# Products that nobody reads in TensorE's waits, a shorter root, a second context buffer, and a wait moved to its write

## What is computed

```python
# layer 0
x = x + cross_attention_0(ln(x), ctx, mask0)     # 16 heads of 16, logits tanh(u)*10, keys and values are ctx itself
x = x + self_attention_0(ln(x))                  # 16 heads, q and k normalised per head (rms), softmax over 256 keys
x = x + ternary_linear(ln(x))                    # weights to -1/0/1, rows to 8 bit integers, one 256x256 product
# layer 1
x = x + cross_attention_1(ln(x), ctx, mask1)     # q, k, v projected; softmax over 4096 keys
x = x + causal_attention(ln(x))                  # 16 heads of 64
x = x + ffn(ln(x))                               # latent attention (4 heads), router, top 2 of 8 experts + a shared one
```

## Time and profile before

| | |
|---|---|
| three runs | 779.72, 775.89, 775.08 us, median 775.89 |
| the profiled execution | 776.85 us, of which its span in the trace is 775.1 |
| PE busy | 619.4 us, 80% of the span |
| PE weight loads | 381.6 us, 49% |
| DVE busy | 417.9 us, 54% |
| ACT busy | 464.7 us, 60% |
| POOL busy | 71.7 us, 9% |
| mean granted clock of TensorE | 0.913 of full |
| DMA | 73.41 MB, mean 95 GB/s |

### The profile page before, as it was taken

One profiled execution on the slowest core, in us unless ns is written; L12 is line 12 of the kernel. 1 busy time (PEld: TensorE's weight loads), 2 busy tenths in 40 slices (PEclk: granted clock), 3 DMA queues, 4 the chain that ended last, 5 costly groups with the idle time before them and its releaser, 6 DMA issues. The chain is left out here.

```text
span 775.1 us, 14282 instructions
## 1 busy us (share of the span) xinstructions
PE 619.4 (80%) x4872; PEld 381.6 (49%) x4872; DVE 417.9 (54%) x921; ACT 464.7 (60%) x558; POOL 71.7 (9%) x148
## 2 busy tenths in 40 slices
PE   2696768788878876497369999999998699845997
PEld 1353434444444343275235555555554567634886
DVE  6564541322322314765578898988982436345443
ACT  3896959999999964273036676776776047203010
POOL 3010201000100003000110101111110100000000
PEclk9998979999999985699568999999999599979799
DMA  5877754476443104000622222332220900000000
GB/s 132 217 215 221 247 174 114 129 206 185 121 119 112 48 22 148 0 1 1 222 65 63 86 80 78 86 79 81 85 63 1 336 30 2 1 0 1 1 0 14
DMA packets 52695, 73.41 MB, mean 95 GB/s; under 512 B 10866, under 2 KB 29618, under 8 KB 52658
## 3 DMA queue, kind: packets, MB, share of 16 engines
q1 hardware_dynamic: 51890, 72.19, 31.7%
q10 hardware_dynamic: 768, 0.73, 0.3%
HBM read 58.89 MB, written 12.85 MB: 93 GB/s over the span
## 5 line engine op out<-in xcount | busy, mean ns | idle before, releaser
L1550 DVE TENSOR_REDUCE sb_m_blk<-ps 128x1 f32<-128x512 f32 x256 | 159.6, 684 | 22.1 <-PE ps L1408 20.9
L1359 ACT ACTIVATE sb_probs<-ps 128x1024 f32<-128x1024 f32 x128 | 125.9, 1025 | 52.5 <-PE ps L1438 51.3
L644 ACT ACTIVATE sb_probs<-ps 128x1024 f32<-128x1024 f32 x128 | 124.0, 1017 | 24.9 <-PE ps L690 22.3
L648 ACT ACTIVATE sb_probs<-sb_probs,sb_neg_cap,sb_cap 128x4096 f32<-128x4096 f32 x32 | 121.6, 3801 | 1.1
L707 PE MATMUL ps<-sb_probs,sb_v_st 128*32 128x256 f32 x1024 | 77.0, 398 | 38.3 <-ACT sb_probs L648 38.3
L1408 PE MATMUL ps<-sb_k_st,sb_q_m 96*128 96x512 bf16 x256 | 91.1, 400 | 2.7 <-DVE sb_m_blk L1550 2.1
L690 PE MATMUL ps<-sb_q_st,sb_k_st 112*128 112x256 bf16 x512 | 76.8, 286 | 5.2 <-DMA sb_k_st<-k_parts_l 4.0
L1438 PE MATMUL ps<-sb_q_st,sb_k_st 115*128 115x256 bf16 x512 | 77.7, 275 | 1.4 <-ACT sb_probs L1359 1.4
L690 PEld LDWEIGHTS ps<-sb_q_st,sb_k_st 112*128 112x128 bf16 x512 | 46.4, 101 | 49.4 <-ACT sb_probs L644 23.9
L1454 PE MATMUL ps<-sb_probs,sb_v_st 128*32 128x256 f32 x1024 | 67.4, 384 | 0.2 <-ACT sb_probs L1359 0.2
L1438 PEld LDWEIGHTS ps<-sb_q_st,sb_k_st 115*128 115x128 bf16 x512 | 49.3, 98 | 19.2 <-issue 2.5
(11 more groups left out here) (254 smaller groups left out, 825.1 us busy)
## 6 DMA issues: line engine op xcount, KB each, us to landing
sb_k_st<-k_parts_l SPq DMA_DIRECT2D x223, 64.0 KB, 2.0
sb_k_st<-k_parts_l SPq DMA_DIRECT2D x93, 128.0 KB, 3.1
k_parts_l<-sb_v_proj SPq DMA_DIRECT2D x24, 256.0 KB
k_parts_l<-sb_early SPq DMA_DIRECT2D x48, 128.0 KB
sb_v_proj<-ctxT_blocks SPq DMA_DIRECT2D x8, 512.0 KB, 8.3
sb_early<-ctxT SPq DMA_DIRECT2D x8, 512.0 KB, 3.8
sb_v_rows<-ctx_by_pair SPq DMA_DIRECT2D x7, 512.0 KB, 4.3
sb_k_st<-k_parts_l SPq DMA_DIRECT2D x64, 32.0 KB, 1.7
```

Of the source, the lines that this page charges most:

```text
L644: a.activation(probs[:, j % 2, 4 * g:4 * g + 4, :], scores_bank(g), ACT.Tanh).then_inc(s["tanh"], 1)
L648: a.activation(probs[:, j % 2], probs[:, j % 2], ACT.Exp, bias=k.neg_cap[:, 0:1], scale=k.cap[:, 0:1]).then_inc(s["exp"], 1)
L1359: sc.activation(probs[:, g], scores_bank(g), ACT.Exp).then_inc(s["exp"], 1)
L1550: v.tensor_reduce(k.m_blk[:, b, q, blk:blk + 1], k.ps[:, m_bank(m_turn_of(idx)), :], AX.X, ALU.max).then_inc(s["m_read"], 1)
```

## The change

- `rsqrt` takes the first guess y, and then t = v*y*y and y times a polynomial of t, written as two quadratic factors: eight instructions where there were ten, two of them issued beside another one.
- `keep_busy(k, n, bank)` issues n matmuls of 128x512 in float32 (ones, and the columns of the output weights `w1_o`) to a PSUM bank that nobody reads then. It stands ahead of waits of TensorE: 5 in `update_pe` where a norm follows (stages two and four), 8, 4 and 8 in stage two, 4 ahead of the flag's load in stage three, 2, 9 and 5 in stage four. It waits for nothing itself.
- A second context buffer `ctx_two` takes the block of pair 1, the normalised rows `xn` and `xnT` of the later stages lie in the same memory. The copies are issued in another order: pair 1 right behind the second key load for pair 1, pair 2 where that of pair 1 stood. `next_ctx(2)` for pair 3 stays.
- VectorE's wait for the stored blocks 6 and 7 goes from the loop's entry into `v_rows` for j = 2 of the loop.

```diff
 RSQRT_MAGIC = float(0x5F3759DF)
+RSQRT_POLY = (0.27406409802012394, (-0.9034915739820695, 1.7067952240054962), (-4.242021545393216, 5.265408709688565))
...
     k.rs_t = k.sb("rs_t", [P, 64])
-    k.xn = k.sb("xn", [P, QT, D])
-    k.xnT = k.sb("xnT", [P, KT, S])
+    k.rs_z = k.sb("rs_z", [P, 64])
+    k.rs_w = k.sb("rs_w", [P, 64])
+    k.ctx_two = k.sb("ctx_two", [P, KT, CBLK])
+    k.xn = k.ctx_two[:, 0, :].rearrange("p (t d) -> p t d", t=QT)
+    k.xnT = k.ctx_two[:, 1, :].rearrange("p (t q) -> p t q", t=KT)
     k.o_nat = k.sb("o_nat", [P, QT, D])
...
-    v, y, t = k.rs_v[:, 0:n], k.rs_y[:, 0:n], k.rs_t[:, 0:n]
+    v, y, t, z, w = (buf[:, 0:n] for buf in (k.rs_v, k.rs_y, k.rs_t, k.rs_z, k.rs_w))
     vec = k.nc.vector
+    (a1, b1), (a2, b2) = RSQRT_POLY[1:]
     link(vec.tensor_scalar(y.bitcast(I32), v.bitcast(I32), -0.5, RSQRT_MAGIC, ALU.mult, ALU.add))
-    for _ in range(3):
-        link(vec.tensor_tensor(t, y, y, ALU.mult))
-        link(vec.scalar_tensor_tensor(out=t, in0=t, scalar=-0.5, in1=v, op0=ALU.mult, op1=ALU.mult))
-        link(vec.scalar_tensor_tensor(out=y, in0=t, scalar=1.5, in1=y, op0=ALU.add, op1=ALU.mult))
+    link(vec.tensor_tensor(t, y, y, ALU.mult), vec.tensor_scalar(z, y, RSQRT_POLY[0], None, ALU.mult))
+    link(vec.tensor_tensor(t, t, v, ALU.mult))
+    link(vec.scalar_tensor_tensor(out=w, in0=t, scalar=a1, in1=t, op0=ALU.add, op1=ALU.mult),
+         vec.scalar_tensor_tensor(out=y, in0=t, scalar=a2, in1=t, op0=ALU.add, op1=ALU.mult))
+    link(vec.scalar_tensor_tensor(out=z, in0=w, scalar=b1, in1=z, op0=ALU.add, op1=ALU.mult))
+    link(vec.scalar_tensor_tensor(out=y, in0=y, scalar=b2, in1=z, op0=ALU.add, op1=ALU.mult))
...
         "proj", "v_copied", "kd_ops", "kd_split", "q_rows", "q_turned", "q_first", "q_stack", "keep",
-        "v_first", "ctx_pair", "first_hi", "first_res", "first_mid")}
+        "v_first", "ctx_pair", "two_in", "first_hi", "first_res", "first_mid")}
     k_in = [k.sem(f"a_k_in{j}") for j in range(4)]
...
                 load_first(1, j)
+            sp.dma_start(k.ctx_two[:, :, :], ctx_blocks[:, :, CBLK:2 * CBLK]).then_inc(s["two_in"], 16)
             store_block(2)
...
                 store_kd1(0, j)
-            next_ctx(0)
+            sp.wait_ge(s["proj"], 4)
+            sp.dma_start(k.ctx_blk[:, :, :], ctx_blocks[:, :, 2 * CBLK:3 * CBLK]).then_inc(s["blk_in"], 16)
             load_first(1, 3)
...
                 sp.wait_ge(s["scores"], 16 + 4 * (j + 1))
-                if j == 3:
-                    next_ctx(1)
                 load_first(2, j)
...
-            def project(it, j, first):
+            def project(it, j, first, second=False):
+                ctx = k.ctx_two if second else k.ctx_blk
                 if j == 0:
-                    pe.wait_ge(s["blk_in"], 16 * (it + 1))
+                    if second:
+                        pe.wait_ge(s["two_in"], 16)
+                    elif first:
+                        pe.wait_ge(s["blk_in"], 16)
+                    else:
+                        pe.wait_ge(s["blk_in"], 16 * it)
                     if first:
...
                     for c in range(KT):
-                        last = t.matmul(k.ps[:, bank, :], k.wk1[:, c, j * P:(j + 1) * P], k.ctx_blk[:, c, :],
+                        last = t.matmul(k.ps[:, bank, :], k.wk1[:, c, j * P:(j + 1) * P], ctx[:, c, :],
                                         start=(c == 0), stop=(c == KT - 1))
...
                         for c in range(KT):
-                            last = t.matmul(k.ps[:, bank, m * D:(m + 1) * D], k.ctx_blk[:, c, ch * P:(ch + 1) * P], k.wv1[:, c, :],
+                            last = t.matmul(k.ps[:, bank, m * D:(m + 1) * D], ctx[:, c, ch * P:(ch + 1) * P], k.wv1[:, c, :],
                                             start=(c == 0), stop=(c == KT - 1))
...
                     if not first:
-                        project(it, j, False)
+                        project(it, j, False, fresh)
                     elif j >= 2:
...
-            def v_rows(it, j):
+            def v_rows(it, j, over_parts=False):
                 dve.wait_ge(s["proj"], 4 * it + j + 1)
+                if over_parts:
+                    for n in (6, 7):
+                        dve.wait_ge(k.sem(f"k0_stored{n % 2}"), blocks_stored(n))
                 v.tensor_tensor(k.v_proj[:, bass.ds(4 * it + 2 * (j - 2), 2), :],
...
                     else:
-                        v_rows(it, j)
+                        v_rows(it, j, block_of is None and j == 2)
                     if block_of is not None:
...
             body(1, FIRST_LATE)
-            for n in (6, 7):
-                dve.wait_ge(k.sem(f"k0_stored{n % 2}"), blocks_stored(n))
             with dve.Fori(2, H // 2) as it:
...
+def keep_busy(k, n, bank):
+
+    for _ in range(n):
+        k.nc.tensor.matmul(k.ps[:, bank, :], k.ones_sq[:, :], k.w1_o[:, :, :].rearrange("p t n -> p (t n)"), start=True, stop=True)
+
+
 def update_pe(k, pe, tag, src, n_k, w, turn, norm=True):
...
     if norm:
+        keep_busy(k, 5, 6)
         pe.wait_ge(k.sem(tag + "_xn"), QT)
...
             t.matmul(k.ps[:, 7, 0:1], k.ones_sq[:, :], k.w_sum[:, :], start=True, stop=True).then_inc(k.sem("c_w_total"), 1)
+            keep_busy(k, 8, 6)
             pe.wait_ge(k.sem("b_qkn"), QT)
...
             last.then_inc(k.sem("b_qkT"), 1)
+            keep_busy(k, 4, 6)
             pe.wait_ge(k.sem("b_kT"), 1)
...
+            keep_busy(k, 8, 6)
             pe.wait_ge(k.sem("c_aq"), 1)
...
+            keep_busy(k, 4, 6)
             masked = pe.value_load(k.masked_i[0:1, 0:1], min_val=0, max_val=1)
...
             small_pe(k, pe, causal)
+            keep_busy(k, 2, 0)
             pe.wait_ge(k.sem("e_oT"), 1)
...
+            keep_busy(k, 9, 0)
             pe.wait_ge(k.sem("f_xn"), QT)
...
+            keep_busy(k, 5, 0)
             pe.wait_ge(k.sem("g_xn"), QT)
```

## The result

The changed kernel takes 749.44 us (median of four runs, 745.07 to 750.28) against 775.49 for the kernel before: the ratio is 0.9638, 95% interval 0.9599 to 0.9677. The profiled execution took 750.28 us, its span is 748.6.

What follows compares the result with a forecast made beforehand. Bounds: ScalarE's pace and two gaps in stage one, then VectorE's chain in TensorE's waits and half clock behind them. -4.9 + 1.4 + 0.2 - 13.5 - 10.0 = -26.8 on 776.85: 750.0, median forecast 749.1, range 744 to 754.

Steps and rivals of the forecast that it cites:

- Root, -4.9: Nine reciprocal roots on VectorE, eight of them gaining: 0.6 us each on two columns, 0.7 for the 64-column one.
- Products, overruns, +1.6: Five-product fills of stages two and four start at half clock and overrun their waits, +1.4 us; near fits elsewhere, +0.2.
- Products, clock, -13.5: Fills keep TensorE at full clock behind its waits, saving 13.5 us of 35.40 us busy in eight half-clock stretches.
- The term for the router: At 716.7, full clock saves 0.9 to 4.2 us, since the clock may fall in eight-column products; 2.8 taken.
- Context buffer, -10.0: First stage: both TensorE waits for context copies go; unit 10 starts at about 105.6 instead of 115.61, bounds 5.3 to 16.0.
- Rival A: First stage gives some 3 us instead of 10, copies being limited by the 16 engines: 756 us; chance 0.14.
- B: First stage: block 7 arrives in time and the full 16.0 us go: 743.1 us; chance 0.12.
- C: Stage three: four products ahead of the flag's load hold up load or branch: 752.5 to 756 us; chance 0.11.
- D: Clock falls again behind several fills, or warm-up was small: -7 instead of -13.5, 755.6 us; chance 0.11.
- E: Products run at 1.2 GHz throughout and overrun the waits, slower than before: 803 us; decides from 1.12 us each; chance 0.03.

Runs made afterwards that it cites:

- copy_first: Changed kernel with VectorE dividing head 2 before block 6's split and copying head 3's accumulator before block 7's split: 746.96 us, ratio 0.9635.
- branch8: Changed kernel with eight unread products instead of four ahead of the flag's load in stage three: 748.2 us, ratio 0.9664.
- context_alone: Kernel before with the second context buffer, new copy order and moved wait, without new root or products: 767.39 us, ratio 0.99.
- fills_alone: Kernel before with the eight `keep_busy` calls alone, old root and old first stage: 764.72 us, ratio 0.9855.
- wait_at_loop: Changed kernel with VectorE's wait for stored blocks 6 and 7 put back at its loop's entry: 758.44 us, ratio 0.9782.
- fills_doubled: Changed kernel with twice the unread products in each group: 780.17 us, ratio 1.0058.
- fills_halved: Changed kernel with half the unread products in each group: 750.68 us, ratio 0.9676.
- branch8_q4: As branch8, with four more unread products behind the q projection of stage three: 741.8 us, ratio 0.9582.

## Why the prediction was right, step by step

- **The time.** 749.1 forecast, 749.44 measured; on the profiled executions 750.0 forecast, 750.28. The mechanisms are the forecast's, but an agreement to 0.3 us is luck: the changed kernel's own runs differ by 5 us, and terms below are off by 0.6 (root), 1.3 (overruns) and 2.2 us (router) and in part cancel.
- **Root, -4.9.** One root of two columns takes 1.33 us in the trace (351.63 to 352.96), forecast 1.35; the seven behind stage one that were costed on the path are consistent with the 4.3 said (0.63 where an interval holds nothing else). Mis-sized is the first norm: 0.6 taken, 0.0 found, because I hung the first unit on the split of block 0, and it hangs on a copy of keys that the root doesn't hold up. The root alone measured 4.0.
- **Products, overruns, +1.6.** Almost none in the profiled execution: 0.06 at 592.68 and ahead of the router, 0.2 ahead of the transposes of q and k. The step at fault is where the clock rises behind the output projection: it had risen at 284.2 and by 588, when the products began, so none of them ran at half. In stage two there was room besides, since VectorE's rows hung on the instruction that ends 7.92 us behind the block's start, which I had not seen. The range was not empty: in stage four of copy_first the projection took 3.78 us and the five products 5.12, VectorE's rows were ready at 585.63 and the transposes started at 586.20, 0.6 late; in branch8 it is 0.8.
- **Products, clock, -13.5.** The clock lines of the table above sum to 13.7, less 0.8 given back in the experts and 0.7 in stage three, 12.2, against 13.5 less 1.6 of overruns forecast, 11.9. Place by place it holds for the linear layer of stage two (5.91 to 3.70 us, 2.2 forecast), for the causal projections (2.5 behind 611.8, 2.6 forecast), for the q projection (0). The term for the router is wrong in size: 2.8 taken, 0.6 found. The clock held through the products of eight columns and fell behind them, at about 694, so the half-clock stretch moved into the experts' first products (6.68 us instead of 5.85). The lower bound, 0.9, assumed that it would fall at once; it didn't name that the loss would come behind.
- **Context buffer, -10.0.** Unit 10 at 105.6 forecast, 105.85 found; gap of 5 to 6 us, 5.36; released by TensorE, TensorE by the accumulator's copy, that at 99.86 (99.9). The half-clock projection behind was 3.76 (3.8). The two profiled executions give 10.0 for the whole first stage; the runs of context_alone give 7.8 (6.1 to 9.5), so the size rests on a profile of the kernel before with a long first stage (289.30, against 285.53 for the same code in fills_alone). Not forecast is the second small wait, 2.44 us of TensorE at 91.75 for the division of head 2 behind the split of block 6; it costs ScalarE 1.9 us at unit 9, and since unit 10 hangs on VectorE anyway, nothing behind it. The wait moved to the write is what carries this term: without it 9.0 us are gone (wait_at_loop).
- **Rival A** (the copies limit stage one) and **B** (block 7 in time) fell by the gap itself; block 7 was issued at 85.85 and its split began at 96.00. **C** fell: first transposes 7.3 us from the block's start, as forecast, and 7.2 with eight products queued. The branch is not always alike, though: it takes 6.17 to 6.33 us in thirteen of the profiles and 7.78 in fills_alone, where the transposes came 8.9 us from the start; it began 0.9 us behind the first product there too, so the products didn't hold it up. **D** fell by the runs of fills_alone and by the 12.2 above, though fills_alone's profile alone, with 7.8 us behind stage one, would have fitted it. **E** by the price, 0.86 to 0.89 against a break-even of 1.12; fills_doubled shows that the kernel does become slower than before once the products run past the waits, though at full clock.
- **The weighing against the Trainium skill.** "TensorE: Matmul & The Clock Gate", Part 1, puts the ramp penalty below 1% of a typical kernel's span, an estimated 7.8 us here. The prediction held that figure against the whole gain, and that was a wrong reading: the sentence is about the ramp at the start of a kernel, and this kernel falls back to half clock in eight stretches behind its waits. The clock gave back 12.2 us between the two profiled executions and fills_alone's runs 11.2 (9.4 to 13.1). That is more than 7.8, but it doesn't contradict the page.

## What to carry to other kernels

Read, behind each wait of TensorE, the granted clock of what follows: a chain that goes back and forth between two engines pays for a wait twice. Products that nobody reads cost nothing while they end before the wait does and 0.86 us each past it at full clock; one issued at half clock took 1.85 us (its two records). Half the products lost 1.2 to 3 us of some 11, twice as many lost 31, so size them short rather than long. And check that the wait depends on what you make faster: in stage two it did not.

When a buffer is added for a wait, follow the engine behind it to its next wait first: here the second buffer without the moved wait brought next to nothing (unit 10 at 115.17 instead of 115.61). And after each such gap look for the next one before counting the whole of it; the 5.36 us ahead of unit 10 turned into 3.57 ahead of unit 13, then into waits for keys.

## What the runs showed that I had not expected

The granted clock at one and the same place differs between the profiles of programs that are alike there, and the mean clock between the executions of one program (0.963 to 0.972 for the changed kernel). The output projection of stage four took 3.37 us in the changed kernel's profile and 3.78 in those of copy_first, fills_alone and fills_halved; from the turn ahead of it to the next one it is 9.01 us in the first, 10.4 in copy_first, branch8 and router, and 7.64 in wait_at_loop and branch8_q4. That of stage two took 3.67 in the changed kernel and 1.99 in fills_alone. The runs of the changed kernel differ by 5 us and those of copy_first by 7; the clock at such places and the spread of stage one may be why, which is not shown, as each kernel has one profile. A gain of 2 us in a single profile says little without the intervals around it.

TensorE's sequencer ran far ahead of the array: with 16 records of 128x512 issued (7.11 us) it loaded a flag and began a branch 0.9 us after the first of them had started, and the branch's 6.2 us passed entirely beside them.
